# Numbering the expert results by partition and loading them in two pieces

## The reference, cut to what matters

```python
x = x + tanh(g_xattn) * xattn(ctx, ctx, layernorm(x))
xn = layernorm(x)
probs = softmax(einsum('bsd,ed->bse', xn, gate_w))
topk_probs, topk_idx = top_k(probs, 2)
h = gelu(w1[expert] @ xn + b1[expert])        # 128 -> 512, for both choices
y = w2[expert] @ h + b2[expert]               # 512 -> 128
out = x + tanh(g_ffn) * sum(y * topk_probs, over both choices)
```

## Time and profile before

| | us |
|---|---|
| median of 3 runs | 92.45 |
| lowest, highest | 92.39, 94.13 |
| span of the profiled execution | 91.6 |

### The profile page before, as it was taken

One profiled execution on the slowest core, in us unless ns is written; L12 is line 12 of the kernel. 1 busy time (PEld: TensorE's weight loads), 2 busy tenths in 40 slices (PEclk: granted clock), 3 DMA queues, 4 the chain that ended last, 5 costly groups with the idle time before them and its releaser, 6 DMA issues.

```text
span 91.6 us, 2708 instructions
## 1 busy us (share of the span) xinstructions
PE 75.9 (83%) x812; PEld 66.7 (73%) x812; DVE 65.3 (71%) x307; ACT 57.1 (62%) x174; POOL 51.1 (56%) x82
## 2 busy tenths in 40 slices
PE   4987798865796457999999999999999999999400
PEld 1374476454772455999979999999999999999300
DVE  2179738998999899999987758479885664617360
ACT  4265689974878697569777867765775676440000
POOL 6975498007778777780000387787778756105150
PEclk9999999999555555579999999999999999999998
DMA  1999999791012112541465345511111110078043
GB/s 21 297 388 394 436 443 429 226 304 33 29 58 65 58 58 87 174 124 33 94 139 114 70 118 118 149 57 56 39 32 49 37 47 20 28 219 228 18 125 104
DMA packets 11662, 12.65 MB, mean 138 GB/s; under 512 B 1379, under 2 KB 10615, under 8 KB 11392
## 3 DMA queue, kind: packets, MB, share of 16 engines
q1 hardware_dynamic: 9840, 9.74, 33.5%
q0 software_dynamic: 1120, 2.12, 7.1%
q10 hardware_dynamic: 688, 0.61, 2.4%
HBM read 8.18 MB, written 4.48 MB: 138 GB/s over the span
## 4 chain that ended last, share of the span: by engine, by line
PE 43%; DVE 29%; DMA 15%; issue 4%; SPq 3%; ACT 1%; POOL 1%; POOLq 1%; DVEq 0%
PE bank L828 17%; DMA res<-results 6%; DMA ctx_sb<-in_ctx_t 6%; DVE hot L945 6%; PE bank L810 4%; PE bank L812 4%; PE bank L811 4%; PE bank L654 3%; DMA results<-y_sb,in_rows 2%; PE bank L794 2%; PE bank L703 2%; DVE x L969 2%; DVE w_lo L1071 2%; PE bank L672 2%; DVE stats L976 2%
## 5 line engine op out<-in xcount | busy, mean ns | idle before, releaser
L610 ACT ACTIVATE hid<-bank,wp 128x128 f32<-128x128 f32 x92 | 26.4, 367 | 13.2 <-PE bank L812 13.1
L457 POOL DMA_INDIRECT results<-y_sb,in_rows x19 | 19.2, 1013 | 16.7 <-ACT y_sb L566 10.4
L828 PE MATMUL bank<-w_sb,hid 128*128 (+1 forms) x184 | 25.8, 284 | 0.0
L828 PEld LDWEIGHTS bank<-w_sb,hid 128*128 128x128 f32 x184 | 22.7, 194 | 0.0
L373 POOL DMA_INDIRECT dispatched<-rows,slot x16 | 16.0, 998 | 9.4 <-DVE slot L1038 5.2
L810 PE MATMUL bank<-xs_t,w_hi 128*128 128x128 f16 x76 | 13.7, 219 | 0.0
L811 PE MATMUL bank<-xs_t,w_hi 128*128 128x128 f16 x76 | 13.7, 219 | 0.0
L812 PE MATMUL bank<-xs_t,w_lo 128*128 128x128 f16 x76 | 13.7, 219 | 0.0
L1145 DVE COPY xs_t<-bank 128x256 f16<-128x256 f16 x19 | 5.5, 291 | 8.8 <-PE bank L794 8.7
L810 PEld LDWEIGHTS bank<-xs_t,w_hi 128*128 (+1 forms) x76 | 7.4, 98 | 0.1
L811 PEld LDWEIGHTS bank<-xs_t,w_hi 128*128 (+1 forms) x76 | 7.4, 98 | 0.0
(11 more groups left out here) (174 smaller groups left out, 170.4 us busy)
## 6 DMA issues: line engine op xcount, KB each, us to landing
w_sb<-in_w SPq DMA_DIRECT2D x2, 2048.0 KB, 11.5
in_rows<-dispatched SPq DMA_DIRECT2D x23, 65.0 KB, 2.1
results<-zeros SPq DMA_DIRECT2D x1, 1024.0 KB, 5.2
res<-results SPq DMA_DIRECT2D x4, 256.0 KB, 4.5
dispatched<-pad_rows SPq DMA_DIRECT2D x9, 65.0 KB, 2.9
ctx_sb<-in_ctx_t SPq DMA_DIRECT2D x1, 512.0 KB, 5.5
wp<-in_wpack ACTq DMA_DIRECT2D x1, 342.0 KB, 3.5
results<-y_sb,in_rows POOLq DMA_INDIRECT x19
```

Source lines behind the costliest of these rows:

```text
L457: pool.indirect_dma_start(results_dram, bass.IndirectOffsetOnAxis(ap=in_rows[:].bitcast(U32)[:, t, TARGET:TARGET + 1], axis=0), y_sb[:, t, ...
L610: mm = act.activation(hid[:, t % HIDS, b, :], hid_ps[h % len(hid_ps)][:, (b % HALVES) * P:(b % HALVES + 1) * P], ACT.Gelu_apprx_tanh, bias ...
L828: mm = pe.matmul(to, hid[:, t % HIDS, b, :], w2_sb[:, e, b * P:(b + 1) * P], start=False, stop=b == BLOCKS - 1)
```

## The change

Rows of `results` are numbered p * 16 + t * 2 + k in place of t * 256 + p * 2 + k. All 16 rows of a partition then stand side by side (8 KB). The numbers are made by the iota of `target`, with other steps and as many elements. The list of tokens, which the one-hot matrices are compared with, is made by an iota in the same order (p * 8 + t in the column of tile t, partition p); it has two dimensions in place of one. The view of `results` follows, and the four loads of 1 KB runs become two loads of half of the tiles each, with one run of 4 KB for each partition. The semaphores are two in place of four: chunks 0 and 1 wait for the first, chunks 2 and 3 for the second.

```diff
-        ld_res, ... = [sem(f"ld_res{i}") for i in range(len(chunks))], ...
+        ld_res, ... = [sem("ld_res0"), sem("ld_res1")], ...
-        res_view = results_dram.rearrange("(t p k) d -> p t k d", p=P, k=TOP_K)
+        res_view = results_dram.rearrange("(p t k) d -> p t k d", p=P, k=TOP_K)
...
-            for i, q in enumerate(chunks):
-                sp.dma_start(res[:, q, :, :], res_view[:, q, :, :]).then_inc(ld_res[i], 16)
+            for i in range(2):
+                half = slice(i * HALF, (i + 1) * HALF)
+                sp.dma_start(res[:, half, :, :], res_view[:, half, :, :]).then_inc(ld_res[i], 16)
...
-            pool.iota(target[:], [[TOP_K * P, TILES], [1, TOP_K]], base=0, channel_multiplier=TOP_K).then_inc(iotas, 1)
+            pool.iota(target[:], [[TOP_K, TILES], [1, TOP_K]], base=0, channel_multiplier=TILES * TOP_K).then_inc(iotas, 1)
...
-                    pool.iota(token_i[:], [[1, TOKENS]], base=0, channel_multiplier=0).then_inc(tokens_set, 1)
+                    pool.iota(token_i[:], [[1, TILES], [TILES, P]], base=0, channel_multiplier=0).then_inc(tokens_set, 1)
...
-                pool.wait_ge(ld_res[c], 16)
+                pool.wait_ge(ld_res[c // 2], 16)
...
-                v.wait_ge(ld_res[c], 16)
+                v.wait_ge(ld_res[c // 2], 16)
```

## The result

The changed kernel is slower. Its median is 94.07 us (93.77 to 94.88, 4 runs) against 92.74 us for the kernel before (4 runs); the ratio is 1.015 (95% interval 1.011 to 1.020). Measured again it was 1.011 (1.006 to 1.015). A ratio leaves out the executions that are over 1.5% above the fastest one of their kernel, while medians and ranges are of all of them. The prediction was 91.9 us, with a range of 90.7 to 92.7 and 0.90 on a change of less than 2%; the change is within 2%, but on the other side of zero and outside the range.

A forecast was written before the change was run, and what follows sets the result against it. The end was taken to wait for the load of `res`, with one DMA engine late. Landing at 86.15 moved the last addition from 88.97 to 88.45, gain 0.5 us: span 91.1, plus 0.8, 91.9 us; range 90.7 to 92.7.

The forecast's parts named there:

- What bounds the kernel now: End of kernel: between 80 and 86.8 us it waits only for the load of `res`, one DMA engine late by a fetch.
- The steps on the load's end: Load of `res`: 4 KB packets save 0.4 us, the fetch again stalls one engine at 82.7, second half lands at 86.15.
- rival A: Load of `res`: no engine is late, second half lands at 84.1 or 84.55, gain 1.9 us (90.55); chance 0.18.
- the slow begin: Start of the load of `res`: 0.45 us lost to slow first packets, 150 ns each in the first half microsecond.
- The rule that promises more: Load of `res`: the skill's fit lands 1 MB 4.4 us after first issue, at 84.0, gain 1.9 us; not adopted.
- The sum: Whole kernel: span 91.6 less gain 0.5 is 91.1, plus 0.8 us between span and median run gives 91.9 us.
- Behind the landing: DVE and POOL after the second landing L: last addition ends at L + 2.3, 88.45 against 88.97, gain 0.5 us.
- The least end of 87.05: DVE's last addition: gating until 84.74 keeps the end at 87.05 even if L is earlier; gain at most 1.9 us.
- The first half: First load of `res`: lands at 82.85, DVE's base sum of chunk 0 starts 0.1 late, covered by idle time; cost 0.
- The cover "up to 83.1": Gating of the last slot tile: DVE's 0.37 us idle wait for PE hides a first-half landing as late as 83.1.
- Iota and scatter: Iotas on POOL cost nothing, bound +0.1; scatters at 8 KB pitch cost 0, bounds -0.1 and +0.5 us.
- Rival C: Load of `res`: reads collide on the 8 KB pitch, halving the rate; +1.8 us, 94.3 us; chance 0.06.

The follow-up runs named there:

- 1: The kernel before, measured again with no edit: ratio 0.997 (0.993 to 1.002); profiled execution 94.7 us.
- 13: The kernel before with no edit, one more profile: time 92.54 us, span 90.8 us, last addition 8.09 us behind the first load's issue.
- 14: The kernel before with no edit, another profile: last landing 6.00 us and last addition 8.15 us behind the first load's issue; no ratio given.
- the paused kernel: The changed kernel with a pause of about 2 us ahead of the two loads: halves landed at 3.72 and 6.21 us; no ratio given.
- 6: The kernel before with DVE's base sum of chunk 0 moved behind the gating of the last slot tile: ratio 1.007 (1.003 to 1.012).
- 4: The changed kernel with DVE's base sum of chunk 0 moved behind the gating of the last slot tile: ratio 1.004 (1.000 to 1.009).
- 3: The kernel before with only the merging into two loads and two semaphores, old numbering: ratio 1.002 (0.997 to 1.006), measured again 1.010.
- 5: The changed kernel with POOL's four sums cut to 8 of 128 elements of each row: ratio 0.9945 (0.989 to 1.000).
- 10: The kernel before with POOL's four sums cut to 8 of 128 elements of each row: ratio 0.994 (0.989 to 0.998).
- 2: The kernel before with only the new numbering, four loads and four semaphores kept: ratio 1.002 (0.996 to 1.008), measured again 1.003.

## Why the prediction was wrong, point by point

**The path.** "What bounds the kernel now" read the end as waiting for the last landing, held up by one DMA engine with a fetch. That was true of that execution and of one more (1), not of 13 and 14. The steps on the load's end rest on it: I forecast that the fetch comes "at 82.7 again" and that the second half lands at 86.15, 6.56 us behind the issue. It landed at 5.53. That the fetch keeps its place because the program is the same was the wrong premise: in the kernel before alone it came at 3.1 (twice), 4.24 and 4.36 us behind the issue. The fetch came 4.4 to 4.8 us behind the issue in every profile with two loads but that of the paused kernel, when nearly all data had been moved, and at 4.2 to 4.4 in 6, 13 and 14. So rival A (no engine late) had the load right in kind; its estimate was a landing 4.5 to 5.0 us behind the issue, and the slow begin makes the rest. The 4.4 us of "The rule that promises more" fell short by 1.1 us; the Trainium skill (DMA: Bandwidth & Descriptors, Anatomy of one DMA) gives that fit for one DMA issued by GpSimd, and these are two, issued by SP.

**The baseline.** The sum took 91.6 us as the span that belongs to 92.45 us of time, a gap of 0.8. Every later run lists both, and the gap is 1.7 to 1.9 us: 93.77 with a span of 92.0, 92.54 with 90.8. So the profiled execution of before was, by estimate, one of some 93.4 us, about 1 us longer than the median that I subtracted the gain from. That was a step one could question: a gap of 0.8 had no row of its own. Where no engine is late, before ends at 8.1 us behind the issue (13 and 14), not at 9.4 (this profile and 1).

**Behind the landing.** This step failed, and it is what turned the sign. It put the last addition 2.3 us behind the second landing; measured are 3.8 us. It set the two base sums behind this landing at 0.80 us, and saw that "both DVE and POOL now wait for the same second landing", yet priced nothing for it. Measured: the two base sums took 1.77 us (86.18 to 87.95 in place of the 0.80), and DVE came to them 0.6 us after the landing, held up by the late first half and by its longer sum of chunk 0. Counted over all, the four base sums of DVE take 3.06 us in place of 1.68 (0.42 + 0.83 + 0.98 + 0.83), 1.4 us more, the size of the whole loss. In the profile of before all of them took 0.41 or 0.42, because with four landings the sums of the two engines overlapped little and DVE's began first. The least end of 87.05, "set by DVE itself", was too low by the same term.

**The first half.** Forecast 82.85, 3.26 us behind the issue; measured 4.26. The term that failed is the slow begin, 0.45 us: it was read from 1 KB packets (150 ns in the first half microsecond). 4 KB packets took 430 ns each in a whole microsecond, and the 0.4 us that they save at full speed (160 ns, as forecast) come after it. The cover "up to 83.1" for the gating of the last slot tile (3.51 us behind the issue) was exceeded by 0.75 us, and DVE's second base sum took 0.41 us longer on top; this moved PE's end by 1.0 us (to 7.13 behind the issue), but not the end of the kernel, since DVE had become the bound (4). So "cost 0" was wrong for another reason: behind the first half DVE is never idle again, and the later this half lands, the later the end. From 3 to the change the first half is 0.39 us later and the last addition too.

**What held.** Iota and scatter cost nothing (1.07 us against 1.04; 2.23 against 2.20, and ratio 1.002 with the numbering alone). What the two missing issues bring is singled out by no run. Rival C, reads that collide on the pitch, did not occur: 410 GB/s at 8 KB pitch.

**The account.** From an execution of before without a late engine (13: last addition at 8.09) to the change (9.31) are 1.2 us, and the ratios, 1.011 and 1.015, say 1.0 to 1.4 us. By the profiles it takes two things together. With DVE's sums short the change ends at 7.88 (5), no later than before: so the coincidence of the sums is needed for the loss. The second is the late first half, by an estimate from the rows of the change: if the first half had been in time, DVE's base sum of chunk 2 would start at the second landing, 5.53, and the 3.17 us from there to the last addition (86.18 to 89.35) would end at 8.7, so about half of the loss would stay. No run has the coincidence in full with an early first half. Not settled: why 4 stands a little better than the change in time and not in its profile, and what makes the begin of such a load slow.

## What to carry to other kernels

Several small loads with a semaphore each do more than move bytes: they decide when each engine starts, and here they kept DVE's two-input sums ahead of POOL's. Before merging transfers, write down who starts on each landing, and price a two-tensor sum of DVE that begins after one of POOL's as waiting for it: here 0.83 to 1.00 us in place of 0.42. And before a sum is made against a profiled execution, ask whether it was a usual one: compare its span with the times by the gap that other runs show, and look at any accident on the path (here one DMA engine late by 1.3 us) as something that the next execution may not have.

## What the runs showed of the hardware that I had not expected

A sum of two tensors in SBUF on DVE and one on POOL hold each other up: the one that begins second ends a fixed time behind the end of the first. For DVE this is 0.28 us, in the change (three times) as in 3 and 13, so that its sum took 0.83 to 1.00 us in place of 0.42. For POOL it is 0.6 us (85.34 behind DVE's 84.74 in the change: 0.96 us in place of 0.72). DVE's additions that read one tensor from PSUM stayed at 0.41 to 0.42 us, also beside POOL's L469 in 13. The Trainium skill, SBUF — State Buffer, Who interferes with whom, states that a DVE instruction with two SBUF inputs contends with a GpSimd instruction that reads SBUF, and that of two which contend the one that comes second waits for the other. By that rule, the traces agree, but for a part: behind POOL's end DVE needs 0.28 us more, not its whole 0.42.

A fetch of 16 KB of instructions took one DMA engine for 0.9 to 1.1 us at the end of the load (the change and 3), for 0.9 to 1.5 us ahead of it (1.07 in the earlier trace rows), and for 1.65 to 1.8 us in the two profiles where it fell into the middle of the load; the last landing then came 1.1 to 1.3 us later than in 13 and 14 (7.13 and 7.22 against 5.93 and 6.00 us behind the issue). When it comes varies, with the same program on PE, and the last landing of the four loads of 1 KB runs goes with it: fetch at 3.1 (before and 1), landing 7.1 to 7.2; at 4.24 to 4.42 (13, 14, 6), landing 5.9 to 6.5; at 5.0 (10), landing 5.6.

Loads begin slowly: 1.0 us from issue to the first packet. Then packets of 1 KB took 150 ns in the first half microsecond against 46 at full speed, and packets of 4 KB 430 ns (273 from w2) in about the first microsecond against 160. This was so from a fresh tensor and from an old one, and the longer the runs, the later the first piece of the load was there (2 and 3).
